# Reordered work at the stage crossings and in the opening of a four-layer graph network kernel

## What is computed

```python
# L0, two rounds: softmax-like weights from h W_left, h W_right, masked by adj and its transpose
u = u_left * adj_tri + u_left * diag_mask + u_right * swap(adj_tri)
h = relu(_layer_norm((exp(u) * adj / sum) @ (h @ W_lin.T + b), ln_a, ln_b))
# L1: 12-head attention, scores + beta * adj, masked where adj == 0
# L2, two rounds: a = softmax(h h.T / temper) * adj, normalised; upper, diagonal and lower part
ctx = (attn * upper) @ hl + diag * hs + (attn * lower) @ hr
h = relu(norm(ctx) * g + beta)
# L3: 12-head attention, scores + adj as a bias, then an output projection Wo
```

## Time and profile before

| what | value |
|---|---|
| profiled execution | 2908.89 us, span 2907.1 us |
| median of the runs | 2906.34 us |
| PE / DVE / ACT / POOL busy | 95% / 67% / 36% / 33% of the span |
| granted PE clock, mean | 0.991 |
| DMA | 211.45 MB, mean 73 GB/s |

### The profile page before, as it was taken

The page is one execution under the profiler, slowest core; times in us unless marked ns, Lnnn a source line. Parts: engine busy times, 40 slices in busy tenths (PEclk is TensorE's granted clock), DMA queues, the critical chain, the costliest instruction groups (busy, mean ns, idle before and its releaser), DMA issues.

```text
span 2907.1 us, 64341 instructions
## 1 busy us (share of the span) xinstructions
PE 2761.9 (95%) x26048; PEld 2339.1 (80%) x26048; DVE 1950.7 (67%) x4550; ACT 1036.6 (36%) x1985; POOL 954.9 (33%) x874
## 2 busy tenths in 40 slices
PE   6999999999999999999999999999999899999997
PEld 5888887888877888887888888888887777877776
DVE  4554454555567767768777776777777777777775
ACT  2333433333334444443333332222223344444342
POOL 1222113444443333333111111344344344444443
PEclk9999999999999999999999999999999999999999
DMA  3222332333411211121221232223323101111101
GB/s 91 67 77 77 101 107 73 109 109 109 128 58 49 64 57 49 60 86 57 72 72 54 66 102 82 86 83 104 104 92 99 46 27 49 48 49 49 38 25 36
DMA packets 197320, 211.45 MB, mean 73 GB/s; under 512 B 72736, under 2 KB 197024, under 8 KB 197024
## 3 DMA queue, kind: packets, MB, share of 16 engines
q1 hardware_dynamic: 197024, 207.33, 23.2%
HBM read 131.80 MB, written 75.50 MB: 71 GB/s over the span
## 4 chain that ended last, share of the span: by engine, by line
PE 78%; DVE 12%; issue 5%; ACT 2%; POOL 2%; DMA 1%; SPq 0%; POOLq 0%; DVEq 0%; ACTq 0%
PE psum L675 31%; PE psum L672 28%; DVE v_x L1505 4%; PE psum L723 3%; PE psum L990 3%; PE psum L660 3%; PE psum L840 2%; PE psum L885 2%; PE psum L829 2%; DVE room L1538 2%; PE psum L975 2%; PE psum L739 2%; PE psum L861 1%; DVE room L1554 1%; DVE fast L1376 1%
## 5 line engine op out<-in xcount | busy, mean ns | idle before, releaser
L675 PE MATMUL psum<-fast 128*128 128x384 f32 x5760 | 1097.1, 342 | 56.4 <-DVE v_x L1505 34.7
L675 PEld LDWEIGHTS psum<-fast 128*128 128x128 f32 x5760 | 995.1, 189 | 117.9 <-DVE v_x L1505 45.9
L672 PE MATMUL psum<-fast 128*128 128x512 f32 x3456 | 861.1, 400 | 10.4 <-ACT room L1191 3.7
L672 PEld LDWEIGHTS psum<-fast 128*128 128x128 f32 x3456 | 637.5, 189 | 164.8 <-issue 25.1
L526 POOL TENSOR_TENSOR room<-room 128x768 f32<-128x768 f32 x128 | 188.8, 1475 | 415.0 <-DVE room L1544 259.6
L1645 DVE TENSOR_TENSOR room<-psum,rows 128x384 f32<-128x384 f32 x384 | 212.4, 553 | 134.1 <-PE psum L675 134.0
L1135 ACT ACTIVATE room<-psum 128x512 f32<-128x512 f32 x192 | 114.7, 597 | 391.7 <-PE psum L672 391.7
L660 PE MATMUL psum<-mask,z_sb 128*128 128x128 f32 x1152 | 178.0, 285 | 53.9 <-ACT z_sb L1116 22.6
L1116 ACT ACTIVATE z_sb<-x_ring,negb,rstd 128x384 f32<-128x384 f32 x256 | 167.8, 701 | 120.4 <-DVE negb L1368 120.3
L1505 DVE TENSOR_TENSOR v_x<-psum,rows 64x192 f32<-64x192 f32 x512 | 181.4, 354 | 28.8 <-PE psum L675 23.6
L660 PEld LDWEIGHTS psum<-mask,z_sb 128*128 128x128 f32 x1152 | 130.8, 143 | 84.6 <-issue 36.1
(11 more groups left out here) (96 smaller groups left out, 3573.5 us busy)
## 6 DMA issues: line engine op xcount, KB each, us to landing
x_ring<-x_mid SPq DMA_DIRECT2D x64, 768.0 KB, 4.5
x_mid<-x_ring SPq DMA_DIRECT2D x48, 768.0 KB, 4.1
x_ring<-x_in SPq DMA_DIRECT2D x32, 768.0 KB, 4.6
z_mid<-x_ring SPq DMA_DIRECT2D x32, 768.0 KB, 4.1
z_sb<-z_mid SPq DMA_DIRECT2D x32, 768.0 KB, 6.4
out<-x_ring SPq DMA_DIRECT2D x16, 768.0 KB, 3.9
w_raw<-w_all SPq DMA_DIRECT2D x19, 576.0 KB, 7.1
adjc<-adj SPq DMA_DIRECT2D x64, 128.0 KB, 3.9
```

The source lines that it names most:

```text
L672: mm = nc.tensor.matmul(dst, wpart[s_][:, c, c_out * P:(c_out + 1) * P], hpart[:, c, 0:GT], start=(k == 0), stop=(k == 3 * C - 1))
L675: mm = nc.tensor.matmul(dst[:, 0:H], hpart[:, c, row:row + P], wpart[s_][:, c, :], start=(k == 0), stop=(k == 3 * C - 1))
```

## The change

It reorders work; no arithmetic changes. In the opening the first rows come as two DMAs, DVE waits for the half that it needs, for masks and beta only later, and splits the first weight before the second group's statistics; ACT runs one tiny activation at once, which brings its table load forward; POOL fills `v_x` before its first wait; the load of group 3 waits for the statistics of group 1. On SP, at every crossing, `load_z` now stands ahead of the load of the third weight (only stages 1 and 4 have it). In DVE's body ahead of att1 (`to_next`) the additions of the old group and the weight splits go behind the value copies. In `to_att` ACT does the fourth copy before the scalings and the fifth between them, and DVE spreads the additions over its other work and puts the second value copy before the scores of tile 0 and the last before those of tile 1.

```diff
 SP
-            def body(g, X, Z):
-                if X and X.norm:
+            def body(g, X, Z, loaded=False):
+                if X and X.norm and not loaded:
                     load_z(X, X.index)
...
-            sp.dma_start(x_ring[:, 0], x_view[0][0]).then_inc(ld["x_in"].sem(Group(0, 0, 0)), 16)
+            sp.dma_start(x_ring[:, 0, 0:2], x_view[0][0][:, 0:2]).then_inc(x_half, 16)
+            sp.dma_start(x_ring[:, 0, 2:4], x_view[0][0][:, 2:4]).then_inc(ld["x_in"].sem(Group(0, 0, 0)), 16)
...
             for p in (2, 3):
+                if p == 3:
+                    after(sp, "ag", Group(0, 0, 1), T - 1)
                 load_x(Group(0, 0, p), p)
...
-                    body(g, g + 2 if k < 2 else Group(n + 1, 0, k - 2) if more else None, nxt)
-                    if more and k == 1:
+                    ahead = g + 2 if k < 2 else Group(n + 1, 0, k - 2) if more else None
+                    if k == 2 and more:
+                        if ahead.norm:
+                            load_z(ahead, 0)
                         load_w(n + 1, 2)
+                    body(g, ahead, nxt, loaded=k == 2)
 POOL: the fill of v_x, from behind n_keep_d(first)
             pool.wait_ge(init_done, 1)
+            nc.gpsimd.memset(v_x[:], 0.0).then_inc(v_set, 1)
+            pool.wait_ge(v_set, 1)
+            for e in (0, 1):
+                nc.gpsimd.memset(v_x[e * S:(e + 1) * S, :, :, :, 2 * HD + e:2 * HD + e + 1], 1.0).then_inc(v_set, 1)
+            pool.wait_ge(v_set, 3)
             pool.wait_ge(mask_in, 32)
 ACT, to_att
                 normed(X, 2, 3)
+                a_keep(F, 3)
                 scaled(g, 0, 1)
-                a_keep(F, 3)
+                a_keep(F, 4)
                 scaled(g, 2, 3)
-                a_keep(F, 4)
                 a_keep(F, 5)
 ACT, opening
+            act.wait_ge(init_done, 1)
+            nc.scalar.activation(z_sb[:, 0, 0:T], halfs[:, 1], ACT.Identity).then_inc(warm, 1)
+            act.wait_ge(warm, 1)
             normed(lead, 0, 1, 2, 3)
 DVE, stats_of (and dve.wait_ge(mask_in, 32) leaves the start)
+                    opening = g.n == 0 and g.index == 0
+                    if half == 0 and opening:
+                        dve.wait_ge(x_half, 16)
+                    if half == (1 if opening else 0):
+                        dve.wait_ge(ld["x_in"].sem(g), ld["x_in"].at(g))
                     if half == 0:
-                        dve.wait_ge(ld["x_in"].sem(g), ld["x_in"].at(g))
 DVE, n_body
-                add_x(g, 0, 1, 2)
-                next_w(F, X, 0, 2)
+                to_next = X and X.att
+                if not to_next:
+                    add_x(g, 0, 1, 2)
+                    next_w(F, X, 0, 2)
                 nat(0)
                 if F:
                     n_scores(F)
-                add_x(g, 3)
+                if not to_next:
+                    add_x(g, 3)
...
                     split_h(F, X, 2)
-                next_w(F, X, 1)
-                nat(2, 3)
+                if to_next:
+                    nat(2)
+                    next_w(F, X, 0)
+                    nat(3)
+                    next_w(F, X, 1)
+                    add_x(g, 0, 1, 2, 3)
+                else:
+                    next_w(F, X, 1)
+                    nat(2, 3)
 DVE, to_att
                 a_bias(F)
+                add_x(g, 0, 1)
                 split_h(F, X, 0)
                 a_nat(F, 0)
+                add_x(g, 2)
                 split_h(F, X, 1)
-                add_x(g, 0, 1, 2, 3)
+                add_x(g, 3)
+                a_nat(F, 1)
                 a_soft(F, 0)
-                a_nat(F, 1)
                 split_h(F, X, 2)
+                a_nat(F, 2)
                 a_sums(F, 0)
-                a_nat(F, 2)
+                a_nat(F, 3)
                 a_soft(F, 1)
-                a_nat(F, 3)
 DVE, opening
             shift_of(lead)
+            split_w(0, 0)
             stats_of(lead + 1, 0, 1)
-            split_w(0, 0)
             for c in range(C):
                 split_h(lead + 1, lead, c)
+            dve.wait_ge(mask_in, 32)
             shift_of(lead + 1)
```

More of the change, by code:

```diff
@@ L263, in graph_layers @@
         init_done = sem("init_done")
+        x_half = sem("x_half")
+        warm = sem("warm")
         A = {n: s.at for n, s in st.items()}
@@ L629, in _ @@
             n_keep_d(first)
-            nc.gpsimd.memset(v_x[:], 0.0).then_inc(v_set, 1)
-            pool.wait_ge(v_set, 1)
-            for e in (0, 1):
-                nc.gpsimd.memset(v_x[e * S:(e + 1) * S, :, :, :, 2 * HD + e:2 * HD + e + 1], 1.0).then_inc(v_set, 1)
-            pool.wait_ge(v_set, 3)
             for n in range(len(PHASES)):
@@ L1337, in _ @@
             dve.wait_ge(boot, 1)
-            dve.wait_ge(mask_in, 32)
             def stats_of(g, *halves):
```

## The result

The changed kernel took 2891.56 us (median of 5, 2889.5 to 2891.72) beside 2906.34 for the kernel before in the same comparison: ratio 0.9948, 95% interval 0.9934 to 0.9963, so 14.8 us faster. The forecast was 2886.6, with a range of 2880 to 2894. The profiled execution took 2891.56, span 2889.8; that of before lies 17.3 us above it. First the page's busy times (rows 1 of before), then the busy time by stretch (as the earlier trace rows, each cut at the same PE work, so 4.5 to 17.3 us earlier; columns PE, PEld, DVE, ACT, POOL, granted clock, DMA share, GB/s).

The account below looks back on a forecast made before the run. TensorE (PE), busy 95% of the span, was taken as the bound. Gains of 5.7 (opening) + 0 + 2.1 + 5.4 + 6.5 = 19.7 us, taken from the median 2906.34, gave 2886.6 us, range 2880 to 2894.

Parts of the forecast that it names:

- the fill: Opening, second half: moving POOL's fill of v_x shortens PE's wait and removes half clock; 3.7 us, bounds 2.6 and 4.6.
- `load_z`: Into the second convolution stage: the early load ends PE's wait and half clock; 5.4 us, bounds 4.5 and 5.8.
- ACT's copy in the last crossing: Into the last attention stage: fourth projection copy ahead of the scalings puts PE 5.9 us earlier at the next part.
- The first attention crossing: From the second graph stage into the first attention stage: 2.1 us earlier, bounds 0.5 and 3.5.
- The first half's gain: First attention crossing: PE's first key projection starts some 3 us earlier, lost at ACT except 0.2 by the first value part.
- the last crossing: Into the last attention stage: PE's sixth part of the first body 6.5 us earlier, bounds 5 and 8.
- rival (a): Last crossing earns 3 instead of 6.5, as DVE's chain sets it and a new gap lowers the clock; 2890.1 us, chance 0.13.
- The first half of the step: Last crossing: the first activation split waits for two additions and so POOL, leaving DVE's chain 3.6 us earlier, not 5.9.
- a sign of being wrong: Listed signs: second rows landing after 20.5, PE's half clock at the new gaps, or clock falls inside the last stage.
- The opening's first half: First projection earlier by moving weight split 0 into DVE's wait for the second rows; 2.0 us, bounds 1.6 to 2.1.
- the "give or take 1" of the forecast: Opening: its 5.7 us in all could vary by 1 with where PE's clock rises at its first projection.
- Two places gained that the forecast had at 0: Crossing near 430: 0, bounds 0 and 0.5; crossing at 1366, with no edited line: 0.

Follow-up runs that it names:

- experiment 9: Changed kernel, last crossing: additions 0 and 1 just ahead of the second value copy; opening: activation splits ahead of the second group's statistics; 2889.16 us.
- experiment 10: Changed kernel with the first rows in one load instead of two halves; 2890.09 us.
- experiments 2 to 4: Kernel before with one edit each: load_z ahead of the third weight load, 2899.80 us; ACT's new order, 2902.66; DVE's new body and crossing orders, 2902.42.
- 5: Changed kernel with DVE's additions 0 and 1 behind the first copy of h and first value copy in both crossings into attention; 2891.87 us.
- 6: Changed kernel with DVE's old order in the crossing into the last attention stage alone; 2887.97 us.
- 8: Changed kernel run again, unaltered; 2892.15 us.
- 11: Changed kernel with DVE's old order in the last body of the second graph stage; 2892.74 us.
- 12: Changed kernel with DVE's old order inside the crossing into the first attention stage; 2890.66 us.

## Why the prediction was right, and where it was not

**The sum by places** held: in the changed kernel each edit earned at its own place, and of the rest only three short places moved (below). Right by mechanism and size are the fill (3.7, measured 3.78), `load_z` (5.4, 5.63) and ACT's copy in the last crossing (5.9, 5.88 at the next part). For the fill I had weighed the Trainium skill (SBUF — State Buffer, "Who interferes with whom"), by which the gain would be near 2.6, since the later of a VectorE cast and a GpSimd operation waits for the whole of the earlier. The cast at 48.84 does look blocked, ending 0.28 behind the end of the POOL row that runs from 48.40 for 1.12; but that neighbour is short, the cast takes 0.96, and 3.78 is earned.

**The first attention crossing** (2.1, measured 1.64) is right at its end and only partly on the way. I kept the shift of the next group at its old time, give or take 1: with the lead of 6.07 taken off it is 0.3 later (851.71 against 857.45). The first half's gain, 4.6 and not 3, is not all lost at ACT: 1.4 goes at the wait for the weight split, which I had not priced, 1.5 at ACT, and 1.5 is left at the first value part where I had 0.2. The part behind the second value copy is 1.9 earlier and not 2.9. These two errors didn't matter, since the chain that I had named as the last, tile 1's scores up to the mixing step, does end last: 2 forecast, 1.6 measured. That they left the sum so near is in part luck.

**The term that was mis-sized is the last crossing**: 6.5, with the bound at 5, measured 3.28. That is rival (a), 3. The first half of the step was right up to the first value copy, "3.6 earlier": it is 3.7 earlier (2239.39 with 13.97 of lead against 2257.05). The step that failed is the next one, "the scores of tile 1 end some 4 earlier": they start 1.2 earlier. The two rows of the kernel before:

```profile
2257.05 1.46 DVE L1505 TENSOR_TENSOR v_x<-psum,rows 64x192 f32<-64x192 f32 x4 [0.88 <-PE psum L675]
...
2271.74 1.09 DVE L1538 SCALAR_TENSOR_TENSOR room<-psum,adjc 128x256 f32<-128x256 f32 x3
```

I let the second value copy go ahead of the scores and costed only the scores' 2.9 us on DVE. Left out was that this copy has to wait for PE's second value part, which follows the first copy and now a gap of 3.89, so that it runs at half clock: 2.39 of idle DVE with the scores behind it. From those scores on DVE's work up to the shift sets the turn that PE waits for (experiment 9). The gap before the last value part came as forecast (2.4; 2.40 before 2252.68), but with the half clock behind it (nine 512-wide matmuls in 4.08 at 2256.76), which I had named only as a sign of being wrong.

**The opening's first half** was 2.0 and is about 1. In the changed kernel's profile the first projection did start 1.87 earlier, and its later rise of the clock took 1.1, the "give or take 1" of the forecast. In the mean of the six runs with the split load the start is 1.5 earlier than in the kernel before, in five with the old opening 0.3, so the move itself is worth 1.2 and not the whole split: the second rows land later. I had taken 0.1 off for the two DMAs and the later issue. The prediction weighed the rule of the Trainium skill (SBUF — State Buffer, "Summary: rules for kernel authors") that one DMA is better than several; experiment 10 agrees with it as far as one run can (19.61 against a mean of 20.2). The cost is likely some 0.8 us on the rows behind, not the 2 by which this half would have been worth 0.

**Two places gained that the forecast had at 0**, 1.5 and 1.2 us, and one lost 0.5. Those near 430 and 1366 are the clock: the gap is the same, but what follows runs at another level. Near 1366 the gap is 3.06 in both, and the same matmuls behind it take 6.53 at a granted clock of 0.50 before and 5.28 at 0.68 behind the change. The loss near 2168 is a wait for a load of `z_sb`, 2.64 before and 3.01 behind the change; over all runs it is 1.61 to 3.24, also in kernels that edit nothing near it. PE at the crossing near 430, before, changed, and experiment 9:

```profile
436.36 3.35 PE L672 MATMUL psum<-fast 128*128 128x512 f32 x9 [2.14 <-issue]
```

```profile
431.81 2.33 PE L680 MATMUL psum<-fast 128*128 128x512 f32 x9 [2.14 <-issue]
```

```profile
429.42 3.44 PE L680 MATMUL psum<-fast 128*128 128x512 f32 x9 [2.11 <-issue]
```

**From profile to median.** The sum of 17.3 is 2.4 below the forecast's, and the other 2.5 of the miss come from the last step: I took 19.7 off the median of 2906.34, though the durations were those of an execution 2.55 above it. The changed kernel's profile lies on its median, so of the 17.3 us between the profiles 14.8 are between the medians. Read the other way, the five places that I had forecast a gain for make 15.1 instead of 19.7, and the last crossing (3.2) and the opening's first half (1.2) are nearly all of that miss; the three others make 2.2. Whether these 2.2 are what the profiled execution of before had lost against its median is open: there is one profile of it, and experiments 2 to 4 lie 3.0 above, 0.8 below and 0.2 above their own medians.

## What to carry to other kernels

Where several engines wait for one another in a crossing, find the chain that ends last before moving work between the others: here an order that served PE's value copies cost 3 us because the scores, and all of DVE's work after them, stood behind them, and the order with PE's longest wait was the best. A copy that is moved ahead of independent work brings its own wait with it; price the wait of the moved instruction, not only its duration. And take a gain from a profile only against its own time: if an execution lies above its median by 2.5 us, part of what it shows as lost is not lost in the median execution, and a forecast taken from the median can come out too low by as much. The same holds for sums of experiments that are all counted from one profile.

## What the runs showed of the hardware

**The same gap lowers the clock in one kernel and not in another.** Behind the gap of 2.14 us near 430 the same 25 matmuls take 5.25 us at a granted clock of 0.67 in the kernel before (436.36 to 441.61) and 3.71 at 1.00 in the changed one (431.81 to 435.52). In the kernels with leads of -0.2 to 0.5 there (before, 2 to 4) and in 9 (6.9) the first nine took 2.98 to 3.51 us; in all nine kernels with leads of 3.1 to 6.5 they took 2.29 to 2.33. The two executions of the changed kernel agree (2.33 and 2.31), so a shift of a few us can earn or cost 1.5 us at a place that nobody edited, and the gain of one experiment holds such places too.

**The rise of the clock at the first projection varies between kernels with the same opening**: 6 to 14 of the 54 matmuls come 0.43 us apart instead of 0.23, with no plain relation to when the projection starts (eight from 27.68 before, thirteen from 25.81 and from 26.47 in the two executions of the changed kernel, six from 24.63 in experiment 9). In the six traces with the changed opening (changed, 5, 6, 8, 11, 12) it is 8 to 13, and the projection takes 14.1 to 15.1 us: 1.0 us that no edit explains. In all traces but the first of the changed kernel the record of the granted clock begins only with this rise, so the level ahead of it is read from the spacing, and the 0.97 and 0.94 of the first stretch in the two profiles can't be compared.

**An addition beside POOL costs more than twice its time.** Where POOL's affine steps run, an addition takes 1.13 to 1.30 us and the step behind it 1.19 to 1.21; alone the four of one row take 1.96 us together and a step 1.00. At 2235.38 the addition starts 0.18 behind a POOL step of 1.01 that began at 2235.20 and ends 0.43 behind that step's end. That agrees with the Trainium skill (SBUF — State Buffer, "Who interferes with whom"): the later of the two waits for the whole of the earlier.
